# Self-attention by pairs of heads in tiles of the PE array, with the softmax division moved behind the product, and GpSimd's weight passes cut into eight pieces

## What is computed

```python
def attn(X, ln_w, ln_b, W_in, W_out):          # B=1, S=256, D=512, 16 heads of 32
    Xn = (X - mu) * rsqrt(var + 1e-5) * ln_w + ln_b
    Q, K, V = split(Xn @ W_in, 3)               # each (16 heads, 256, 32)
    Q, K = rope(Q), rope(K)                     # the first 16 channels of a head
    probs = softmax(Q @ K.T / sqrt(32))         # (16, 256, 256)
    return (probs @ V) @ W_out + X

def weight_quant(w):                            # w1, w2, w3 of the feed-forward layer
    scale = 1.0 / clip(mean(abs(w)), 1e-5)
    return clip(round(w * scale), -1.0, 1.0) / scale
def ffn(x):
    h = silu(bitlinear(x, w1)) * bitlinear(x, w3)   # bitlinear quantises rows of x, too
    return bitlinear(h, w2)
```

## Time and profile before

| what | value |
|---|---|
| median of 3 runs | 612.31 us (609.09 to 613.04) |
| profiled execution, its span | 611.09 us, 609.0 us |
| busy over the span: PE, DVE, ACT, POOL | 543.2, 501.3, 378.8, 169.1 us |
| QKV stage | 490.0 to 516.5 us |
| self-attention, from the first score matmul to the residual's | 516.5 to 573.8 us |
| output projection | 573.8 to 582.5 us |
| feed-forward layer | 582.5 to 609.0 us |

### The profile page before, as it was taken

One profiled execution on the slowest core, in us unless ns is written; L12 is line 12 of the kernel. 1 busy time (PEld: TensorE's weight loads), 2 busy tenths in 40 slices (PEclk: granted clock), 3 DMA queues, 4 the chain that ended last, 5 costly groups with the idle time before them and its releaser, 6 DMA issues.

```text
span 609.0 us, 9985 instructions
## 1 busy us (share of the span) xinstructions
PE 543.2 (89%) x3759; PEld 359.7 (59%) x3762; DVE 501.3 (82%) x769; ACT 378.8 (62%) x487; POOL 169.1 (28%) x146
## 2 busy tenths in 40 slices
PE   6989938799989989999999999999979997788896
PEld 3767613266666657666666666666767853355543
DVE  4698858998988888898899998999966656799786
ACT  3154445877767776876767868778785348553332
POOL 0599853001222212212212120210000243455001
PEclk9999988799999999999999999999999999889999
DMA  8976403999999999999999999999997973000000
GB/s 344 328 240 211 129 10 53 168 201 200 209 203 214 200 192 208 208 212 214 204 214 211 210 216 210 211 212 210 206 184 138 396 301 149 0 0 1 2 1 34
DMA packets 287806, 107.40 MB, mean 176 GB/s; under 512 B 276896, under 2 KB 277920, under 8 KB 286368
## 3 DMA queue, kind: packets, MB, share of 16 engines
q1 hardware_dynamic: 287776, 107.01, 80.8%
HBM read 37.26 MB, written 0.52 MB: 62 GB/s over the span
## 4 chain that ended last, share of the span: by engine, by line
PE 47%; DVE 22%; DMA 11%; SPq 8%; issue 5%; POOL 4%; ACT 3%; DVEq 0%; ACTq 0%
DMA pT<-split 10%; PE ps L651 10%; SPq L444 6%; DVE split L1246 6%; PE ps L653 5%; DVE rows L1264 5%; PE ps L633 4%; PE ps L635 4%; PE ps L634 4%; PE ps L755 3%; POOL qrope L484 2%; PE ps L793 2%; DVE anb L1414 2%; PE ps L819 2%; PE ps L698 1%
## 5 line engine op out<-in xcount | busy, mean ns | idle before, releaser
L651 PE MATMUL ps<-pT,VH 128*128 128x256 f16 x1024 | 196.2, 273 | 14.8 <-DMA pT<-split 14.7
L1264 DVE TENSOR_SCALAR_CACHE_REDUCE rows<-ps,qback 128x1024 f32<-128x1024 f32 x128 | 163.6, 1281 | 30.5 <-PE ps L635 30.0
L653 PE MATMUL ps<-pT,VL 128*128 128x128 f16 x1024 | 182.7, 219 | 0.0
L1015 ACT ACTIVATE split<-rows,rz 128x2048 f16<-128x2048 f32 x64 | 124.8, 1994 | 80.6 <-DVE rz L1215 78.2
L1246 DVE SCALAR_TENSOR_TENSOR split<-rows,rz,split 128x2048 f16<-128x2048 f32 x64 | 150.2, 2349 | 1.3 <-ACT split L1015 0.8
L651 PEld LDWEIGHTS ps<-pT,VH 128*128 128x128 f16 x1024 | 100.2, 98 | 64.8 <-DMA pT<-split 28.9
L1001 ACT ACTIVATE rows<-rows,negm 128x2048 f32<-128x2048 f32 x64 | 127.3, 1990 | 10.3 <-DVE negm L1269 10.3
L516 POOL TENSOR_TENSOR ctx_c<-acc 128x128 f32<-128x128 f32 x32 | 36.8, 1151 | 301.1 <-ACT acc L990 301.1
L653 PEld LDWEIGHTS ps<-pT,VL 128*128 128x128 f16 x1024 | 100.4, 98 | 23.4
L633 PE MATMUL ps<-KH,qcur 128*128 128x512 f16 x256 | 98.8, 386 | 9.4 <-DVE qcur L1319 4.6
L634 PE MATMUL ps<-KL,qcur 128*128 128x512 f16 x256 | 98.7, 385 | 0.0
(11 more groups left out here) (182 smaller groups left out, 774.5 us busy)
## 6 DMA issues: line engine op xcount, KB each, us to landing
w_sb<-w SPq DMA_DIRECT2D x3, 2816.0 KB, 16.4
wq_sb<-wq SPq DMA_DIRECT2D x4, 1024.0 KB, 9.9
wo_sb<-wo SPq DMA_DIRECT2D x16, 256.0 KB, 3.5
wkcq_sb<-wkcq SPq DMA_DIRECT2D x4, 768.0 KB, 6.3
keys<-ctxT SPq DMA_DIRECT2D x8, 256.0 KB, 3.4
stage<-ctxT SPq DMA_DIRECT2D x16, 128.0 KB, 4.1
stage<-kcos SPq DMA_DIRECT2D x8, 256.0 KB, 4.0
stage<-ksin SPq DMA_DIRECT2D x8, 256.0 KB, 5.0
```

The costliest lines, as they stand in the source:

```text
L651: nc.tensor.matmul(bank(6 + r % 2, 0, 256), VH[:, 4 * b + k, :], p.rearrange("p x q -> p (x q)"), start=(b == 0 and k == 0), stop=False)
L653: last = nc.tensor.matmul(bank(6 + r % 2, 0, 128), VL[:, 4 * b + k, :], p[:, 0, :], start=False, stop=(b == 7 and k == 3))
L1015: nc.scalar.activation(split[:, split_slot(r, half), :, 0, :], rows[:, k, half * 2048:(half + 1) * 2048].rearrange("p (b k) -> p b k", k=1 ...
L1264: nc.vector.tensor_scalar(rows[:, k, c * 1024:(c + 1) * 1024], ps[:, score_bank(s) * 512:(score_bank(s) + 2) * 512], qback[:, r // 2:r // ...
```

## The change

The self-attention goes by eight units `v` of two heads (`UNITS`) and both token tiles. `kbd` and `vbd` become plain arrays `kT` and `v_sb`, so POOL's two memsets and the copies by head go: DVE makes one copy for each token tile of keys and one for values, ACT none of the keys. The factor 1/sqrt(32) moves into ACT's copy of the queries.

- Scores: four matmuls for a unit, each of 32 rows (one head's channels) and 256 columns, in the row tile of that head; the two heads go to two banks.
- Maxima: one reduction, without the multiplication. The exponentials take the negated maxima as bias, and have no accumulated sum.
- The unscaled exponentials are transposed: two heads of four transposes. DVE copies the first head, ACT the second.
- Products: eight matmuls for a unit, each with 32 columns of weights and 256 moving columns. Two column tiles take the two heads' values, the two others a block of ones, which gives each head's sum of exponentials, repeated over 32 partitions. They share a bank of PSUM.
- `context_out(v)`: DVE takes the reciprocal of the sums, 64 partitions by 256 columns from PSUM, and multiplies the context with it into `cT`.
- PE's order is transposes of `v`, scores of `v` + 2, products of `v` - 1. The rest of the value projection stands ahead of the scores. The clip of `w1` stands in unit 5 of DVE's order, the other two behind the last `context_out`.
- POOL's six passes become 8 instructions of 704 columns each; a clip waits for all eight of its array.

```diff
-        kbd = at("kbd", D + 16 * KB, [128, AH, TOK])
-        vbd = at("vbd", C + 16 * KB, [128, TT, AH, 128])
+        kT = at("kT", D + 16 * KB, [128, FG, TOK])
+        v_sb = at("v_sb", C + 16 * KB, [128, TT, DM])
...
-            nc.gpsimd.memset(vbd[:, :, :, :], 0.0).then_inc(bd_zero, 1)
...
-            nc.gpsimd.memset(kbd[:, :, :], 0.0).then_inc(bd_zero, 1)
...
             def weight_magic(j, wf):
                 pool.wait_ge(wscale_done, j + 1)
-                nc.gpsimd.tensor_scalar(wf[:, :], wf[:, :], wscale[:, j:j + 1], MAGIC, ALU.mult, ALU.add)\
-                    .then_inc(wmagic_done, 1)
+                for k in range(WPIECES):
+                    part = slice(k * DK * FF // WPIECES, (k + 1) * DK * FF // WPIECES)
+                    nc.gpsimd.tensor_scalar(wf[:, part], wf[:, part], wscale[:, j:j + 1], MAGIC, ALU.mult, ALU.add)\
+                        .then_inc(wmagic_done, 1)
...
+            project(1, 2, range(DK // 2, DK))
+
+            def head_scores(v):
+
+                g, first = v // 2, v % 2 * 2
...
+                wait(pe, aexp_done, 4 * (v - 1))
+                for t in range(TT):
+                    for x in range(2):
+                        part = slice((first + x) * DH, (first + x + 1) * DH)
+                        last = nc.tensor.matmul(bank(4 + v % 2 * 2 + x, t * TOK, (t + 1) * TOK), qT[part, t, g, :],
+                                                kT[part, g, :], start=True, stop=True, tile_position=((first + x) * DH, 0))
                 last.then_inc(ascore_done, 1)
...
+            def head_products(v):
...
+                o = (2 + v % 2) * 512 + g % 2 * TOK
                 for k in range(TT):
+                    for x in range(2):
+                        a = first + x
+                        nc.tensor.matmul(ps[a * DH:(a + 1) * DH, o:o + TOK],
+                                         v_sb[:, k, (4 * g + a) * DH:(4 * g + a + 1) * DH], pT[:, a, k, :],
+                                         start=(k == 0), stop=(k == TT - 1), tile_position=(0, a * DH))
+                    for x in range(2):
+                        a = 2 - first + x
+                        last = nc.tensor.matmul(ps[a * DH:(a + 1) * DH, o:o + TOK], ones[:, 0:DH], pT[:, first + x, k, :],
+                                                start=(k == 0), stop=(k == TT - 1), tile_position=(0, a * DH))
                 last.then_inc(aav_done, 1)
...
+            head_scores(0)
+            head_scores(1)
+            for v in range(UNITS):
+                head_transposes(v)
+                if v + 2 < UNITS:
+                    head_scores(v + 2)
...
+                if v >= 1:
+                    head_products(v - 1)
+            head_products(UNITS - 1)
...
+            def exponentials(v):
+                act.wait_ge(anm_done, v + 1)
+                wait(act, apT_done, 2 * (v - 3))
+                for x in range(2):
+                    for t in range(TT):
+                        k = 2 * x + t
+                        nc.scalar.activation(prob[:, v % 4, x, t, :], bank(4 + v % 2 * 2 + x, t * TOK, (t + 1) * TOK),
+                                             ACT.Exp, bias=anm[:, v, k:k + 1]).then_inc(aexp_done, 1)
...
+            def context_out(v):
+
+                g, own, other = v // 2, v % 2 * 64, 64 - v % 2 * 64
+                o = (2 + v % 2) * 512 + g % 2 * TOK
+                dve.wait_ge(aav_done, v + 1)
+                link(nc.vector.reciprocal(arz[own:own + 64, v % 2, :], ps[other:other + 64, o:o + TOK]))
+                nc.vector.tensor_tensor(cT[own:own + 64, g, :], ps[own:own + 64, o:o + TOK], arz[own:own + 64, v % 2, :],
+                                        ALU.mult).then_inc(cT_done, 1)
...
+            value_copies(1)
+            maxima(0)
+            maxima(1)
+            weight_total(1)
+            for v in range(UNITS):
+                probabilities_out(v)
+                if v in (0, 4):
+                    weight_scale(v // 4 + 1, bank(2, 0, 1))
+                if v + 2 < UNITS:
+                    maxima(v + 2)
+                if v == 3:
+                    weight_total(2)
+                if v == 5:
                     clip(0, w1b)
...
+                if v >= 1:
+                    context_out(v - 1)
+            context_out(UNITS - 1)
+            clip(1, w3b)
             clip(2, w2b)
```

More of the change, by code:

```diff
@@ L364, in wo_part @@
             return w[h // (XH // 2)][:, h % (XH // 2), :]
-        def k_rows(copy, t, a):
-            part = slice(a * DH, (a + 1) * DH)
-            return copy(kbd[part, a::HPG, t * 128:(t + 1) * 128], bank(t)[part, :].rearrange("p (g k) -> p g k", g=FG))
         block = ctx.enter_context(nc.Block())
@@ L786, in head_scores @@
                     pe.wait_ge(wmean_done, 1)
-                if u < 2:
-                    pe.wait_ge(qT_done, t + 1)
-                wait(pe, aexp_done, 4 * (u - 1))
-                for a in range(2):
-                    if u == 0:
-                        pe.wait_ge(kbd_done[a], 2 * TT)
-                    last = nc.tensor.matmul(bank(4 + u % 2 * 2 + a), qT[:, t, g, :],
-                                            kbd[:, 4 * g + 2 * a:4 * g + 2 * a + 2, :].rearrange("p h k -> p (h k)"),
-                                            start=True, stop=True)
@@ L796, in head_scores @@
-                last.then_inc(ascore_done, 1)
-            def head_transposes(g, a):
-                pe.wait_ge(prob_done, 4 * (2 * g + 1) + a + 1)
-                wait(pe, pT_done[a % 2], 2 * g + a // 2)
-                for k in range(TT):
-                    for t in range(TT):
-                        o = (k * TT + t) * 128
-                        last = nc.tensor.transpose(bank(a % 2, o, o + 128),
-                                                   prob[:, (2 * g + t) % 4, a, k * 128:(k + 1) * 128], ident[:, :])
-                last.then_inc(apT_done, 1)
@@ L809, in head_product @@
-            def head_product(g, a):
-                if a == 0:
-                    wait(pe, cT_done, g - 1)
-                    if g == 1:
-                        pe.wait_ge(v_copied, 2 * HPG)
-                    if g % 2 == 0:
-                        pe.wait_ge(wmean_done, g // 2 + 2)
-                pe.wait_ge(pT_done[a % 2], 2 * g + a // 2 + 1)
-                for k in range(TT):
-                    last = nc.tensor.matmul(bank(2 + g % 2, 0, TOK), vbd[:, k, 4 * g + a, :], pT[:, a, k, :],
-                                            start=(a == 0 and k == 0), stop=(a == HPG - 1 and k == TT - 1))
-                last.then_inc(aav_done, 1)
@@ new lines, in head_scores, with head_transposes @@
+                for t in range(TT):
[3 more added lines that the diff above has]
+                                                kT[part, g, :], start=True, stop=True, tile_position=((first + x) * DH, 0))
+                last.then_inc(ascore_done, 1)
+            def head_transposes(v):
+                for x in range(2):
+                    pe.wait_ge(aexp_done, 4 * v + 2 * x + 2)
+                    wait(pe, pT_done[x], v)
+                    for k in range(TT):
+                        for t in range(TT):
+                            o = (k * TT + t) * 128
+                            last = nc.tensor.transpose(bank(x, o, o + 128), prob[:, v % 4, x, t, k * 128:(k + 1) * 128],
+                                                       ident[:, :])
+                    last.then_inc(apT_done, 1)
```

179 lines of the change are left out of this document (59 added, 120 removed).

## The result

The changed kernel takes 594.35 us (median of 4 runs, 591.01 to 598.65), beside 612.67 us for the kernel before on the same chip (4 runs, 609.09 to 614.97): ratio 0.971, 95% interval 0.9665 to 0.9755. The forecast was 593.5 in a range of 583 to 609. The profiled execution took 593.24 us, its span is 591.4.

The account below looks back on a forecast made before the run. No engine is full; the chain of waits, with DVE stalled behind POOL's passes (19.8 us), bounds the touched stages. Quantised transposes 22.8 us earlier, 4 taken back for the clock: minus 18.8, 593.5 us on the median, range 583 to 609.

Parts of the forecast that it names:

- The stalls behind POOL: QKV stage and self-attention: DVE instructions with tensor inputs in SBUF stand still until POOL's running instruction ends; 19.8 us lost.
- (1): QKV stage: rotation waits for a 704-column piece, 0.8 us of stall kept; first score at 514.6 against 516.51.
- (3): Work added on DVE per self-attention unit: reciprocal of 64x256 from PSUM 1.75 us, product 0.42 us.
- Rival D: Self-attention on DVE: reciprocal is cheap (0.42 us), DVE needs 2.7 us a unit; minus 28, 584 us; chance 0.08.
- (4): PE in the self-attention: tiles overlap, 2.65 us a unit plus 0.2 for each of three tile-shape switches, 3.25 us.
- Rival B: PE in the self-attention: tiles run one after the other, 6.24 us and switches a unit; 608.8 us; chance 0.13.
- (5): Self-attention to first quantised transposes: DVE's 4.07 us a unit sets time; 22.8 us earlier, 4 back for clock, minus 18.8.
- (6): POOL's passes over the weights: 0.86 us for a piece of 704 columns, sixth pass ends at 550.1.
- Rival A: POOL becomes the end: pieces of 1.27 us, DVE stands at the last clip; minus 8.9, 603.4 us; chance 0.20.
- Rival C: Self-attention on PE: tiles one after the other and clock at 1.2 GHz for half the stage; 625 us; chance 0.07.
- Rival E: POOL's queue keeps DVE out until a whole pass is done; rotation and a clip meet it; about 597 us; chance 0.05.
- The other signs: Include no 128x4 DVE instruction over 0.3 us, rotation's longest product under 1.5, reciprocals 1.6 to 2.2, POOL done before 556.

Follow-up runs that it names:

- the early clip: Changed kernel with DVE's clip of `w1` moved from unit 5 to unit 1: 592.74 us, ratio 0.968.
- one tile: Changed kernel with all matmuls of a unit in the array tile of its first head, products one accumulation after the other: 617.17 us, ratio 1.009.
- all three changes: Changed kernel with division by groups of four heads, clip of `w1` in unit 1, POOL's first pass after the last rotation: 589.36 us, ratio 0.961.

## Why the prediction was right, point by point

**The stalls behind POOL** were read rightly where it mattered, and the two halves of the change add up as measured (6.4 and 11.7 us). The reading was too wide in one point. Not every DVE instruction on operands in SBUF stands still beside POOL: the reciprocals of four sums, SBUF to SBUF, kept their 0.17 us, this one of the kernel before in the middle of POOL's pass of 523.69 to 528.57:

```profile
524.43 0.17 DVE L1404 RECIPROCAL arz<-az 128x4 f32<-128x4 f32 x1
```

The stalled ones were multiplications by a number (`TENSOR_SCALAR`) and the rotation's products and sum of two arrays (`TENSOR_TENSOR`). And the rule that a piece cuts a stall to one piece holds only for single instructions: by itself the cut gave 6.4 of the 19.8 us of stalls. The rest went because the change takes the SBUF-to-SBUF work out of the loop.

**(1) The first score**: forecast 1.9 us sooner, measured 1.2. The term that was off is the rotation's. I kept 0.8 us of stall; each of its instructions met its own piece, and DVE was busy with them for 2.71 us where the undisturbed rotation at 507.73 took 1.26: 1.5 us, inside the bounds of 0 to 2.8. Removing it moved the first score by 0.65 us and the end by nothing that can be seen.

**(3) The reciprocal**: forecast 1.75 us for 64x256, worked out from an instruction of 14 columns; measured 1.76. The estimate of 2.1 us that I had worked out from the repeat count of 8 in VectorE: DVE Perf Modes, section First, the fixed hardware budget, in the Trainium skill, is not borne out by the trace. Rival D (0.42) is out, and its price was too optimistic as well: with the whole division gone the kernel takes 588.2 us, where D had 584. By its own last context D's sum takes off only some 1.5 us for the clock, where the main one takes 4, and it left out POOL: without the reciprocal DVE's last clip waits 2.89 us for it.

**(4) PE**: forecast 3.25 us a unit, measured 3.09. The tiles overlap. TensorEngine Tiling (Array Packing), section Key Properties, in the Trainium skill, has a change of tiling mode drain the array; three changes a unit leave room for 0.44 us together (3.09 - 2.65), less than the 0.6 I had put in. Rival B had 608.8 us; 617.2 were measured, 5.0 of them the clip that was kept out, so the tiles' part was priced 3.4 us too low. The score units did not advance by the 0.43 us a pair that I had named as a sign, but by 0.53 (1.07 for two pairs), the products by 0.43 a quadruple (two steps of 0.21), as named.

**(5) The sum.** From the first copy of `pT` to the last context I had 33.0 us of work, 2 of waiting and 4 for the clock; the trace has 38.2 us (520.53 to 558.73), of which DVE waits 5.5 (1.64, 1.75, 0.66, 0.41 and 1.05). The two clips behind it and the first layernorm took 3.2 and 4.9 us, as said. The clock's 4 us had the right size: keeping the clock up gives 3.6 us in the trace and 4.0 in the medians, and a unit at the lower clock took PE 5.7 us (transposes from 522.68, products ended before 528.43), above DVE's 4.1, as the forecast had it. The size is that of these executions, though: the early clip's trace shows that the first fall of the clock needn't come. The exact agreement of the sum is luck, two misses that cancel: the first copy came 0.9 us later than forecast, and the stretch behind it took 38.2 us where I had 39. (The terms ahead of the first copy add up to 518.2, not to the 518.4 in the text, a slip of 0.2 us.) **-18.7** at the first quantised transpose and -18.8 at the end of the span, against -18.8; it is this exact only after the 1.2 us are taken out by which everything before ran later.

**(6) POOL**: forecast 0.86 us a piece and an end at 550.1; measured 0.75 and 0.83, but the queue waited 4.15 us for the mean of `w2` and lost 1.4 us to the clip, and ended at 554.1. Rival A (1.27 a piece) is out; the clip of `w2` at 560.30 had 6 us of room. A piece of 704 columns at 0.83 us speaks for my reading of the 640-column row of 1.22, that a wait is in it, though no run has that row undisturbed.

**Rival C** had the lower clock for half of the stage. The clock did fall, to a mean of 0.80 from 514 to 556 us, below the 0.88 of the stage before, but C had the matmuls one after the other as well; with the tiles overlapping the lower clock cost some 4 us.

**Rival E** had 0.05 for its effect on the total. That was fair for the profiled execution of the kernel after, and too little for the mechanism: it shows in two of the traces here, where it cost 5.0 and 12.4 us. What decides whether the clip gets in is open. In the kernel after and the one with the early clip it got in between two pieces of a scaling pass, and without the reciprocal that of `w3` into a rounding pass (2.28 us); with one tile it was kept out of a rounding pass, with all three changes out of a scaling pass and the rounding pass behind it.

The other signs that I had named were met, but for DVE as the busiest engine: by busy time POOL and PE are level with it.

## What to carry to other kernels

Look at what an instruction stands next to before you cut the instruction that blocks it: cutting GpSimd's passes gave 6.4 us by itself, and the larger part, 11.7, came with the rest of the change, in which VectorE's operands lie in PSUM and the matmuls in tiles. How much of it is the operands' alone isn't shown; without the tiles nothing of it was left. Heads of 32 channels belong in different array tiles (some 17 us here; the order of the queue made no difference), and a division by rows' sums should be taken over 128 partitions at once (7.0 us less of VectorE's work). A wait of a few microseconds on TensorE is worth filling if matmuls on the critical loop follow it (3 to 4 us here), two profiled executions that differ by a few microseconds should be compared by their clocks first, and where a clip must run between GpSimd's instructions, make GpSimd wait for it.

## What the runs showed of the hardware that I had not expected

- VectorE can be kept out by a row of short GpSimd instructions: 14.05 us for a clip of 1.62 us of work beside 16 pieces, 6.75 beside 8. In the seven other traces in which it began with more than one piece still to come it took 1.63 to 2.28 us. SBUF — State Buffer, section Who interferes with whom, in the Trainium skill, gives the pair to whichever starts first, for the whole instruction; these traces add that one who waits is not next in turn by right.
- Not every VectorE instruction on operands in SBUF stands still beside GpSimd: a reciprocal of 128x4 took its 0.17 us in the middle of a pass, a multiplication of 128x4 by a constant 3.92 (kernel before).
- Four matmuls of 32 rows in two row tiles and eight in four row tiles take the same 1.1 us, and eight products in four column tiles 1.00 us against 3.57 in one.
- The reciprocal's time goes by columns: 64x256 and 128x256 both take 1.76 us.
- After PE waited 2.17 us at 517.7 the granted clock was 0.71 and 0.60 in the next two windows; with the wait filled it was 1.00. The wait alone doesn't decide it: with the same wait unfilled, the clock fell in seven traces and stayed at 1.00 up to 530 us in two, those of the early clip and of all three. What decides is open.
